# Cross-attention and feed-forward block on one core: float16 split products, and normalised activations turned by transposing DMAs

## The reference

```python
x = x + _L0_xattn_ref(_layernorm(x), ctx, mask, wq, bq, wk, bk, wv, bv, wo, bo)
x = x + _L0_ffn_ref(_layernorm(x), w_freq_real, w_freq_imag, ffn_bias)
# xattn: q = x@wq+bq, k = ctx@wk+bk, v = ctx@wv+bv, 16 heads of 32
score = jnp.einsum('bhqd,bhkd->bhqk', q, k) / sqrt(32)
score = score * mask
score = jnp.where(score == 0, -1e9, score)
context = jnp.einsum('bhqk,bhkd->bhqd', softmax(score), v)
return context.reshape(B, Qs, D) @ wo_w + wo_b
# ffn: real(ifft(fft(x) @ w)) + bias, along the last axis
```

## Time and profile before

| | us |
|---|---|
| median of 3 runs | 511.56 |
| lowest, highest | 510.26, 512.6 |
| span of the profiled execution | 510.0 |
| busy: PE, DVE, ACT, POOL | 492.7, 424.9, 369.5, 337.0 |

### The profile page before, as it was taken

How to read it: one execution, slowest core, us unless ns; L and a number is a source line. 1 busy time by engine, 2 the same in 40 slices (tenths; PEclk the granted TensorE clock), 3 DMA queues, 4 the chain that set the end, 5 groups by cost and what they waited for, 6 DMA issues and landing times.

```text
span 510.0 us, 11110 instructions
## 1 busy us (share of the span) xinstructions
PE 492.7 (97%) x3576; PEld 389.9 (76%) x3576; DVE 424.9 (83%) x724; ACT 369.5 (72%) x1420; POOL 337.0 (66%) x497
## 2 busy tenths in 40 slices
...
GB/s 309 415 194 242 116 7 109 2 91 26 120 36 84 75 64 83 64 72 69 89 53 103 55 86 49 77 82 59 71 76 37 64 53 53 63 42 23 22 41 62
DMA packets 46728, 43.78 MB, mean 86 GB/s; under 512 B 4816, under 2 KB 35152, under 8 KB 46032
## 3 DMA queue, kind: packets, MB, share of 16 engines
...
## 4 chain that ended last, share of the span: by engine, by line
PE 86%; POOL 4%; DVE 4%; issue 2%; ACT 2%; DMA 1%; SPq 0%; POOLq 0%; DVEq 0%
PE bank L299 49%; PE bank L396 10%; PE bank L304 8%; PE bank L413 6%; PE bank L384 5%; PE bank L348 3%; PE bank L367 3%; PE bank L409 2%; DMA xs<-in_x 1%; ACT zs L465 1%; DVE zs L572 1%; POOL x L704 1%; POOL x1n L702 1%; DVE nmin L584 1%; POOL sm L698 1%
## 5 line engine op out<-in xcount | busy, mean ns | idle before, releaser
L465 ACT ACTIVATE zs<-zs,nbias 128x128 f32<-128x128 f32 x512 | 200.2, 401 | 9.1 <-POOL nbias L715 8.4
L465 ACT ACTIVATION_READ_ACCUMULATOR zs<-zs,nbias 128x1 f32 x512 | 100.7, 197 | 0.0
L572 DVE TENSOR_TENSOR zs<-bank,ms 128x512 f32<-128x512 f32 x128 | 82.1, 683 | 1.4 <-POOL ms L709 0.7
L715 POOL TENSOR_SCALAR nbias<-nmin 128x8 f32<-128x8 f32 x64 | 15.8, 246 | 101.9 <-DVE nmin L584 92.6
L579 DVE SCALAR_TENSOR_TENSOR zs<-zs 128x1024 f32<-128x1024 f32 x64 | 79.3, 1240 | 0.9
L299 PE MATMUL bank<-xth,wqh 128*128 128x256 f32 x256 | 75.5, 295 | 2.1 <-DVE xtl L535 2.1
L584 DVE TENSOR_REDUCE nmin<-zs 128x8 f32<-128x1024 f32 x64 | 77.2, 1206 | 0.0
L299 PE MATMUL bank<-xth,wql 128*128 128x256 f32 x256 | 72.4, 283 | 0.0
L299 PE MATMUL bank<-xtl,wqh 128*128 128x256 f32 x256 | 72.3, 283 | 0.0
L474 ACT COPY pt<-bank 128x512 f32<-128x512 f32 x128 | 68.5, 591 | 0.2 <-PE bank L396 0.2
L396 PE MATMUL bank<-ident,zs 128*128 128x128 f32 x512 | 66.7, 273 | 1.5 <-ACT zs L465 1.5
...
## 6 DMA issues: line engine op xcount, KB each, us to landing
...
qs<-qh SPq DMA_DIRECT2D x128, 64.0 KB, 2.0
...
qs<-ql SPq DMA_DIRECT2D x64, 64.0 KB, 2.0
...
```

Of the source, the lines that this page charges most:

```text
L465: last = act.activation(z, z, ACT.Exp, bias=nbias[:, s % 4, i:i + 1], scale=-NEG, accum_out=zsum[:, s % 4, i:i + 1])
L572: dve.tensor_tensor(zs[:, s % NZ, t], A[n % 2][:].rearrange("p (h k) -> p h k", h=4), ms[:, c % NM, t, :].unsqueeze(1).broadcast_to([128, ...
```

## The change

- All split parts are float16 instead of float32r. The weights are scaled: wq by SQ = 8, wo and M by SO = 16. bq is multiplied by 8 on POOL, the mask's factor is divided by 8, and after WO and FF the sum on DVE multiplies by 1/16 in the same instruction.
- The XT and T2 fills are gone from PE, with ACT's casts and DVE's subtractions that followed them. Instead ACT casts xn to `xnh` (`norm_hi1`, end of slot r = 3) and x1n to `x1nh` (`norm_hi2`, end of r = 1 and 2); POOL makes `xnl` (`norm_lo1`, r = 0) and DVE `x1nl` (`norm_lo2`, r = 2 and 3), all in token layout. SP then issues transposing DMAs: `turn_xn`, two of 128x1024, at r = 0; `turn_x1n`, two of 128x512, at r = 2 for tile 0 and at r = 3 for tile 1. xth and xtl are now double. Q waits for the first, FF for the second.
- Q moves from the head of its slot to its end, as the last thing on PE; its `hi` and `lo` are at the head of the next slot. WO and FF follow PT.
- Six buffers for x1 instead of four.

The core of the diff:

```diff
-MASK_SCALE = 1e-9 / 32.0 ** 0.5
+MASK_SCALE = 1e-9 / 32.0 ** 0.5 / 8.0
...
-NO = 4
+NO = 6
+SQ = 8.0
+SO = 16.0
...
-        g = {
-            0: [("Q", c + 1, 1), ("WO", c - 2, 0), ("XT", c + 2, 0)],
-            1: [("XT", c + 2, 1), ("WO", c - 2, 1)],
-            2: [("T2", c - 2, 0), ("Q", c + 2, 0), ("FF", c - 3, 1)],
-            3: [("T2", c - 2, 1), ("FF", c - 2, 0)],
+        mid = {
+            0: [("WO", c - 2, 0)],
+            1: [("WO", c - 2, 1)],
+            2: [("FF", c - 3, 1)],
+            3: [("FF", c - 2, 0)],
         }[r]
-        g = [f for f in g if 0 <= f[1] < NC] + early.get(v, [])
+        mid = [f for f in mid if 0 <= f[1] < NC] + early.get(v, [])
+        late = {0: [("Q", c + 1, 1)], 2: [("Q", c + 2, 0)]}.get(r, [])
+        late = [f for f in late if 0 <= f[1] < NC]
...
+        items += [("G", n) for n in mids]
...
+        items += [("G", n) for n in lates]
+        slots[v] = (items, held, mids)
+        held = lates
...
+def turn_slot(c):
+    return norm_slot(c) + 1
...
-        xth, _ = sb("xth", [128, 4, CH], F32R)
-        xtl, _ = sb("xtl", [128, 4, CH], F32R)
-        wqh, _ = sb("wqh", [128, 4, D], F32R)
-        wql, _ = sb("wql", [128, 4, D], F32R)
-        woh, _ = sb("woh", [128, 4, D], F32R)
-        wol, _ = sb("wol", [128, 4, D], F32R)
-        mh, _ = sb("mh", [128, 4, D], F32R)
-        ml, _ = sb("ml", [128, 4, D], F32R)
+        xnh, _ = sb("xnh", [128, 2, D], F16)
+        xnl, _ = sb("xnl", [128, 2, D], F16)
+        xth, _ = sb("xth", [128, 2, 2, 4, 128], F16)
+        xtl, _ = sb("xtl", [128, 2, 2, 4, 128], F16)
+        wqh, _ = sb("wqh", [128, 4, D], F16)
+        wql, _ = sb("wql", [128, 4, D], F16)
...
+            def turn_xn(c):
+                sp.wait_ge(h1_done, c + 1)
+                sp.wait_ge(p_l1, 2 * c + 2)
+                if c >= 2:
+                    sp.wait_ge(g_done, at["Q", c - 2, 1] + 1)
+                for src, dst in ((xnh, xth), (xnl, xtl)):
+                    sp.dma_start_transpose(dst[:, c % 2].rearrange("p t k n -> p (t k) n"),
+                                           src[:].rearrange("p t d -> p (t d)")).then_inc(d_t1[c % 2], 16)
+
+            def turn_x1n(c, t):
+                n = tile_of(c, t)
+                sp.wait_ge(l2_done, n + 1)
+                if c >= 1:
+                    sp.wait_ge(g_done, at["FF", c - 1, t] + 1)
+                for src, dst in ((x1nh, x1h), (x1nl, x1l)):
+                    sp.dma_start_transpose(dst[:, t], src[:, t]).then_inc(d_t2[t], 16)
...
+                if r == 2 and 0 <= c - 2 < NC:
+                    turn_x1n(c - 2, 0)
+                if r == 3 and 0 <= c - 2 < NC:
+                    turn_x1n(c - 2, 1)
+                for a in range(NC):
+                    if turn_slot(a) == v:
+                        turn_xn(a)
                 if r == 1 and 0 <= c + 1 < NC:
                     stack_q(c + 1)
...
-                elif kind == "XT":
-                    pe.wait_ge(p_n1, 2 * c + 2)
-                    for i in range(2):
-                        for t in range(2):
-                            a = 256 * i + 128 * t
-                            k = 2 * f + i
-                            last = pe.transpose(o[:, a:a + 128], xn[:, t, 128 * k:128 * k + 128], ident[:])
                 elif kind == "Q":
                     pe.wait_ge(w_lo, 2)
-                    pe.wait_ge(g_free, at["XT", c, 1] + 1)
+                    pe.wait_ge(d_t1[c % 2], 32 * (c // 2 + 1))
                     for i in range(2):
                         g = slice(128 * (2 * f + i), 128 * (2 * f + i) + 128)
-                        last = split_mm(o[:, 256 * i:256 * i + 256],
-                                        [((wqh[:, k, g], wql[:, k, g]), (xth[:, k, :], xtl[:, k, :]))
+                        last = split_mm(o[:, 256 * i:256 * i + 256].rearrange("p (t n) -> p t n", t=2),
+                                        [((wqh[:, k, g], wql[:, k, g]), (xth[:, c % 2, :, k, :], xtl[:, c % 2, :, k, :]))
...
-                elif kind == "T2":
-                    pe.wait_ge(p_n2, tile_of(c, f) + 1)
-                    for k in range(4):
-                        last = pe.transpose(o[:, 128 * k:128 * k + 128], x1n[:, f, 128 * k:128 * k + 128], ident[:])
                 elif kind == "FF":
-                    pe.wait_ge(g_free, max(at["T2", c, f], at["M", 3]) + 1)
+                    pe.wait_ge(g_free, at["M", 3] + 1)
+                    pe.wait_ge(d_t2[f], 32 * (c + 1))
...
+                if kind == "M":
+                    last = act.activation(mh[:, c, :], src[:], ACT.Identity, scale=SO)
...
+            def norm_hi1(c):
+                act.wait_ge(p_n1, 2 * c + 2)
+                if c >= 1:
+                    act.wait_ge(d_t1[(c - 1) % 2], 32 * ((c - 1) // 2 + 1))
+                act.copy(xnh[:], xn[:]).then_inc(h1_done, 1)
+
+            def norm_hi2(c, t):
+                n = tile_of(c, t)
+                act.wait_ge(p_n2, n + 1)
+                if c >= 1:
+                    act.wait_ge(d_t2[t], 32 * c)
+                act.copy(x1nh[:, t], x1n[:, t]).then_inc(h2_done, 1)
...
+                if r == 1 and 0 <= c - 2 < NC:
+                    norm_hi2(c - 2, 0)
+                if r == 2 and 0 <= c - 2 < NC:
+                    norm_hi2(c - 2, 1)
+                for a in range(NC):
+                    if norm_slot(a) == v:
+                        norm_hi1(a)
...
-                    last = dve.tensor_tensor(x1[:, n1 % NO, :], src[:], xs[:, c % NX, f, :], ALU.add)
+                    last = dve.scalar_tensor_tensor(out=x1[:, n1 % NO, :], in0=src[:], scalar=1.0 / SO,
+                                                    in1=xs[:, c % NX, f, :], op0=ALU.mult, op1=ALU.add)
...
+            def norm_lo2(c, t):
+                n = tile_of(c, t)
+                dve.wait_ge(h2_done, n + 1)
+                dve.tensor_tensor(x1nl[:, t], x1n[:, t], x1nh[:, t], ALU.subtract).then_inc(l2_done, 1)
...
+                if r == 2 and 0 <= c - 2 < NC:
+                    norm_lo2(c - 2, 0)
+                if r == 3 and 0 <= c - 2 < NC:
+                    norm_lo2(c - 2, 1)
...
-                    pool.wait_ge(g_done, at["XT", c - 1, 1] + 1)
+                    pool.wait_ge(h1_done, c)
+                    pool.wait_ge(p_l1, 2 * c)
...
+            def norm_lo1(c):
+                pool.wait_ge(h1_done, c + 1)
+                if c >= 1:
+                    pool.wait_ge(d_t1[(c - 1) % 2], 32 * ((c - 1) // 2 + 1))
+                for t in range(2):
+                    pool.tensor_tensor(xnl[:, t], xn[:, t], xnh[:, t], ALU.subtract).then_inc(p_l1, 1)
...
+                for a in range(NC):
+                    if turn_slot(a) == v:
+                        norm_lo1(a)
```

96 lines of the change are left out of this document (45 added, 51 removed).

## The result

The changed kernel takes 560.11 us (median of 4 runs, 558.21 to 562.73), the kernel before 511.79 on the same chip: a ratio of 1.096, interval 1.092 to 1.100. It is slower, as forecast, but by 48 us where 12 were forecast, and its median lies just over the upper end of the range, 560. The profiled span is 556.7 us against 510.0.

The account below looks back on a forecast made before the run. PE bounds the kernel before at 27.7 us a chunk; afterwards Sync's loop does. Span 510.0 - 29.8 (turns) - 15 (pitch) + 14 (start) + 1 (end) + 42 (loop) = 522.2; as a median 524 us, range 486 to 560.

Parts of the forecast that it names:

- TensorE's relief: Turns leave TensorE (1.86 us a chunk) and split products start closer (0.94 us): 24.9 us a chunk instead of 27.7.
- The start: Before the first scores: first Q near 34 us, longer wait 11, slow restart 2, qs copies 1; plus 14 us.
- T1: Sync's issue of one 128x1024 turn of xn, taken as 1.8 us.
- T2: Sync's issue of one 128x512 turn of x1n, taken as 1.0 us.
- landing: Time for a DMA's data to arrive after its issue, taken as 2.0 us.
- The loop that decides: Per chunk through stack_q, ACT's qh and exponentials, POOL's xnl and Sync's turns: 28.15 us, giving back 42 us.
- rival B: Turns on Sync cost what their bytes say or more: 540 to over 600 us, clock may fall; chance 0.20.
- End: plus 1: After the last x1n, cast, subtraction, turn and landing come some 2 us later, partly under FF: plus 1 us.
- Hidden as busy time, but in a bad place: POOL's subtraction for xnl, 2 x 1.28 us a chunk: hidden in POOL's 22.6 us, but standing in Sync's loop.
- A: Turns on Sync as cheap as plain copies: loop of 25.6 us, 491 us; chance 0.30 together with C.
- C: DVE instead of Sync sets the pace, 25.6 us a chunk with waits for qh: 491 us; 0.30 with A.
- D: New types bring no better pitch on PE: costs nothing with the 28.15 us loop, 504 us in case A.

Follow-up runs that it names:

- e11_no_xnl_sub: e7_q_first with GpSimd's subtraction for xnl left out and the high part of xn turned twice: 495.4 us, ratio 0.970.
- e1_types_only: Kernel before with only the float16 split parts and scaled weights, all turns staying on TensorE: 493.2 us, ratio 0.965.
- e3: Changed kernel without a chunk's three turns of low parts, the products reading the high part instead: 529.3 us, ratio 1.039.
- e4: Changed kernel with eight copies in stack_q instead of twelve from chunk 2 on: 533.8 us, ratio 1.045.
- e12: Changed kernel with GpSimd's subtraction for xnl left out and the high part of xn turned twice: 522.9 us, ratio 1.025.
- e2: Changed kernel with xn's statistics, norm and parts made up to three slots sooner and its turn issued a slot sooner: 549.9 us, ratio 1.076.
- e13_filler: Changed kernel with eight added 512-column products on TensorE under the wait for x1n in FF of tile 0: 552.5 us, ratio 1.080.
- e9_x1n_by_dma: e1_types_only with x1n alone turned by DMA, xn still turned on TensorE: 489.1 us, ratio 0.956.
- e7_q_first: Changed kernel with xn made and turned earlier and Q back at the head of its slot: 521.5 us, ratio 1.020.

## Why the prediction was wrong

The forecast was 524 us with a range up to 560, and the kernel takes 560.11. The loop and its pace were right. Wrong were the clock, the first chunks and the end; they come under "The steps that failed".

**TensorE's relief** was right and a little small: 24.9 us a chunk forecast, 24.58 measured once nothing else bounds (e11_no_xnl_sub), of which the types gave 1.41 and not 0.94 (e1_types_only).

**The start** was right. The first Q starts at 36.06 (34 forecast), the first scores 14.5 us later than before (14 forecast). The rows of TensorE and its windows:

```profile
36.06 0.37 PE L337 MATMUL bank<-xth,wqh 128*128 128x256 f16 x1 [17.75 <-DMA xtl<-xnl]
```

```profile
36.00:41.10 5.10, 5.04 (x24) 3.55 (x25) 0.00 (x0) 1.04 (x1) 3.97 (x4) 0.50 0.09 18
44.80:47.40 2.60, 2.60 (x25) 2.33 (x24) 0.69 (x1) 0.00 (x0) 2.52 (x3) 1.00 0.00 0
```

After 17.75 us without work the first Q runs at a granted clock of 0.50, the 1.2 GHz level, and takes 5.1 us, the next one at 1.00 takes 2.6: the 2 us that the forecast gave for this are there as 2.5.

**The turn's price.** T1 was taken as 1.8 us and is 1.24 to 1.34; T2 was taken as 1.0 and is 1.20 to 1.27; landing was taken as 2.0 and is 2.4 to 2.5 for x1n, 3.2 for xn (medians). A turn of 128x1024 thus costs Sync hardly more than one of half the size: neither the price by bytes holds nor that of plain copies (0.60). The estimate of 1.7 us from the table of the Trainium skill, DMA: Bandwidth & Descriptors, Why a DMA increments its semaphore by 16 and not by 1, which scales with the tiles, is refuted in its scaling: twice the tiles cost 0.1 us. Nor was the other sentence cited, in Advanced Engine Details and Errata of the Trainium skill, X-Bar Transpose (TRN2), a guide to the issue: turns as fast as regular DMAs would have been issued in 0.60 us, not 1.2 to 1.3. At T1 near 1.3 the prediction set the point at which the time is that of before; the kernel is 48 us slower with T1 at 1.3. That the errors in T1, T2 and landing nearly cancel is luck: the loop through Sync, the one by FF, is 27.72 us in an undisturbed chunk, where the prediction had 27.9 for it and 28.15 for the one by qh, which it used.

**The loop that decides.** The mechanism, a loop through Sync and FF or qh, is shown (the chain after; e3 and e4 shorten it by other means and gain 31 and 26 us), and its signs came: TensorE busy for 90% of an undisturbed chunk, FF and qh waiting for their DMAs. Its pace is not what the prediction missed by, since an undisturbed chunk is 0.43 us shorter than forecast. What it had wrong here is what would hold without this loop: TensorE alone at 24.9 us. It costed Q's lo at the head of the slot with "some 0.5 us each" on VectorE and did not follow who waits behind it: zero_to_neg, cn, and by cn the products on TensorE ahead of the next Q. With Sync's loop shortened or opened a chunk still takes 26.3 to 27.8 us (e12, e3, e4, e2).

**The steps that failed.** The sum fell 34.5 us short of the measured span, by stretches 0.5 at the start, 13.8 in chunks 0 to 3, 10.3 in chunks 4 to 13 and 9.9 in the end.

The first is the clock, which the prediction kept for rival B ("the clock may fall") and left at nothing in its sum, though the same sum has TensorE idle for 3.25 us in each chunk (2.7 in the undisturbed one). It accounts for about all of the 10.3 us: the five chunks of 4 to 13 at full clock last 27.94 us on average, under the 28.15 forecast, and the five at a lower one 30.44. With the gaps filled and the clock at 1.00 in all ten (e13_filler) they take 282.4 us, and the forecast's figure for them is 277.3 + 4.3 = 281.6.

The second is that it let the chunks of the start run at the pace of the steady ones, and chunk 0 faster still, with TensorE's whole relief. Chunk 0 takes 29.12 us where 24.17 - 2.8 = 21.4 were forecast, chunk 2 takes 32.20 where 25.7 were; chunks 1 and 3 come within 0.6. The chain of waits through chunk 0:

```profile
57.75 5.55 DMA lp<-in_lparts
...
63.37 3.23 POOL lp L796 x2
...
67.95 3.22 POOL xnl L741 x2
...
71.22 1.25 SPq L259
```

The last load of lp goes out behind the first stack_q, at 57.75 (40.95 in the kernel before). GpSimd has to work on it before it comes to the low part of xn, and the turn of xn and the next stack_q wait for that. In chunk 2 TensorE waits 2.39 us for wol and 1.92 for cn, and then has a low clock:

```profile
138.39:145.58 7.19, 7.19 (x43) 4.76 (x44) 3.05 (x6) 3.24 (x13) 6.41 (x12) 0.61 0.49 110
```

The 24 products of Q in it take 4.65 us and 2.74 at full clock. No run changes these two chunks alone; without GpSimd's subtraction (e12_after_no_xnl_sub) they take 2.1 and 3.2 us less and the four chunks 8.7, and the rest was read from the trace and not tested.

The third is "End: plus 1", with the relief kept in the last chunks. In e9_x1n_by_dma, where nothing but x1n is turned by DMA, the end is 6.9 us longer than in e1_types_only, and 5.2 of these go when the last chunk alone is turned on TensorE. The way of a turn that FF waits for (cast, subtraction, two issues of 1.2, landing 2.5) has no cover once the slots run out, and the wait of 4.4 us costs clock besides.

**GpSimd's subtraction.** "Hidden as busy time, but in a bad place" is right for this kernel: the sum had it in the loop with 2.56 us, it is 2.29 there. What it takes from VectorE beside it was not in the sum; that matters little here (24.41 us of VectorE's time in an undisturbed chunk, 24.0 forecast) and most where VectorE is full, 26 us in e7_q_first.

**The rivals.** A (turns cheap): no, they cost twice a plain copy. B (540 or more, clock falls): its time came, but not by its cause, since T1 was under the forecast; its remark on the clock was right. C (VectorE): false for the kernel as it is, 24.4 of 27.7 us; but it is what bounds next once the loops are open (26.3 of 26.4 in e7_q_first), at a price that e11_no_xnl_sub and the durations put down to contention. D (no better pitch): refuted by e1_types_only. Its 504 is also a slip: without the pitch TensorE needs 25.8 us a chunk and the loop of 25.6 gives nothing back, so the terms of the sum give 497.
